# Moving work between VectorE and GpSimd in the opening of a gated attention and feed-forward block, with side operands in PSUM

## What is computed

```python
# step 1: x and the context are quantised to 0..255, then multiplied
q = clip(round(v / s + z), 0, 255);  fake_quant(v) = (q - z) * s
x = x + tanh(g_xattn) * (fake_quant(layernorm(x)) @ fake_quant(ctx))      # ctx: 2 x 1024 x 1024
# step 2: feed-forward with quantised activations and weights
g = max(|a|) / (448 * 6)
A = blockwise fp8 of (a / g), blocks of 16; the last 128 columns twice: value, and what rounding left
W = blockwise int4 of the weights: s = max|w| / 7 per block of 16, round(clip(w / s)) * s
h = silu(A @ Wg.T * g) * (A @ Wu.T * g)                                   # 2752 columns
y = quantised(h) @ Wd.T * g_h
x = x + tanh(g_ffn) * y
```

## Time and profile before

| | us |
|---|---|
| median of 3 runs (892.26 to 893.98) | 892.41 |
| the profiled execution | 893.12 |
| its span, first to last instruction | 891.3 |
| PE busy | 744.3 (84%) |
| DVE busy | 639.3 (72%) |
| POOL busy | 306.9 (34%) |
| ACT busy | 293.8 (33%) |

### The profile page before, as it was taken

How to read it: one execution, slowest core, us unless ns; L and a number is a source line. 1 busy time by engine, 2 the same in 40 slices (tenths; PEclk the granted TensorE clock), 3 DMA queues, 4 the chain that set the end, 5 groups by cost and what they waited for, 6 DMA issues and landing times.

```text
span 891.3 us, 10314 instructions
## 1 busy us (share of the span) xinstructions
PE 744.3 (84%) x3479; PEld 337.1 (38%) x3483; DVE 639.3 (72%) x993; ACT 293.8 (33%) x351; POOL 306.9 (34%) x175
## 2 busy tenths in 40 slices
PE   1697004198589999999999999999699899999998
PEld 0243002044234444444444444444234344444443
DVE  6989999998546575757566675643489999989810
ACT  5753543333214242435252433420122221121100
POOL 2331416525326484757475766640000000000000
PEclk9899557599799999999999999999999999999999
DMA  8630556343478879888987979770524557654420
GB/s 321 224 116 1 116 214 136 67 100 71 105 179 167 192 171 194 172 210 194 203 176 188 217 168 232 169 158 24 197 36 119 129 152 175 141 141 127 112 58 24
DMA packets 228612, 131.37 MB, mean 147 GB/s; under 512 B 201568, under 2 KB 212832, under 8 KB 227552
## 3 DMA queue, kind: packets, MB, share of 16 engines
q1 hardware_dynamic: 228576, 130.92, 60.2%
HBM read 61.88 MB, written 19.66 MB: 91 GB/s over the span
## 4 chain that ended last, share of the span: by engine, by line
PE 68%; DVE 20%; DMA 3%; SPq 2%; issue 2%; ACT 2%; POOL 2%; DVEq 0%; ACTq 0%
PE acc L1096 43%; PE acc L1148 23%; DVE big L1477 1%; DVE bst L1192 1%; SPq L422 1%; DVE h_in L1293 1%; DVE big L1487 1%; DMA mid<-wbuf 1%; DVE big L1479 1%; DVE big L1486 1%; PE acc L1051 1%; DVE w_max L1269 1%; DVE big L1488 1%; POOL big L667 1%; DVE big L1225 1%
## 5 line engine op out<-in xcount | busy, mean ns | idle before, releaser
L1096 PE MATMUL acc<-mid 128*128 128x512 f16 (+1 forms) x2112 | 455.4, 379 | 69.9 <-DMA mid<-big 63.1
L1096 PEld LDWEIGHTS acc<-mid 128*128 128x128 f16 x2112 | 208.8, 99 | 316.2 <-issue 51.2
L1148 PE MATMUL acc<-big,mid 128*128 128x512 f16 x1056 | 232.1, 383 | 9.7 <-DMA mid<-wbuf 8.5
L1148 PEld LDWEIGHTS acc<-big,mid 128*128 128x128 f16 x1056 | 103.7, 99 | 137.5 <-issue 9.1
L706 POOL TENSOR_TENSOR h_in<-wbuf,h_in 128x1024 f16<-128x1024 f32 (+1 forms) x56 | 114.5, 2044 | 107.4 <-ACT h_in L954 107.3
L656 POOL TENSOR_TENSOR wbuf<-wbuf,w_inv 128x1024 f32<-128x1024 f32 (+1 forms) x67 | 129.4, 1939 | 51.6 <-DVE w_inv L1275 51.6
L1506 DVE SCALAR_TENSOR_TENSOR h_out<-acc,gs,silu 128x256 f32<-128x256 f32 (+1 forms) x88 | 41.8, 475 | 124.6 <-ACT silu L881 101.1
L1269 DVE TENSOR_REDUCE tb<-wbuf 128x64 f32<-128x1024 f32 (+1 forms) x60 | 70.3, 1172 | 44.3 <-DMA wbuf<-in_L_ffn_w_gate_dram 28.7
L781 ACT ACTIVATE wbuf<-wbuf 128x1024 f32<-128x1024 f32 (+1 forms) x67 | 68.0, 1016 | 97.8 <-POOL wbuf L656 97.1
L954 ACT ACTIVATE h_in<-wbuf 128x1024 f16<-128x1024 f32 (+1 forms) x56 | 57.0, 1019 | 114.8 <-DVE wbuf L1281 114.8
L1281 DVE SCALAR_TENSOR_TENSOR wbuf<-wbuf,tb 128x1024 f32<-128x1024 f32 (+1 forms) x60 | 69.8, 1166 | 0.2
(11 more groups left out here) (155 smaller groups left out, 525.8 us busy)
## 6 DMA issues: line engine op xcount, KB each, us to landing
h_in<-h_d SPq DMA_DIRECT2D x8, 1376.0 KB, 7.0
wbuf<-in_L_ffn_w_gate_dram SPq DMA_DIRECT2D x21, 512.0 KB, 4.3
wbuf<-in_L_ffn_w_up_dram SPq DMA_DIRECT2D x21, 512.0 KB, 4.3
h_d<-h_out SPq DMA_DIRECT2D x80, 128.0 KB, 3.4
big<-in_ctx_dram SPq DMA_DIRECT2D x16, 512.0 KB, 5.1
wbuf<-in_L_ffn_w_down_dram SPq DMA_DIRECT2D x16, 512.0 KB, 4.4
big<-in_x_dram SPq DMA_DIRECT2D x8, 512.0 KB, 5.8
x_d<-big SPq DMA_DIRECT2D x8, 512.0 KB, 4.1
```

Source lines behind the costliest of these rows:

```text
L1096: last = pe.matmul(acc[m % 4][:, 0:cols], left[:, k, s * P:(s + 1) * P], ring[:, slot, right, k, 0:cols], start=(k == 0 and left is a_hi a ...
L1148: last = pe.matmul(acc[2 * i + hf][:], amT[:, i, k // DH, left, k % DH, :], right[:, k, hf * MW:(hf + 1) * MW], start=(k == 0 and left == ...
```

## The change

Outside the tail's small changes, only the opening is rewritten:

- `clip_ctx` leaves VectorE; GpSimd clips and shifts all 16 context tiles (`clip_shift_ctx`).
- `back_open` of the 11 opening pieces leaves VectorE. ScalarE subtracts the rounding constant (`whole_w`, a new pass), GpSimd multiplies the block scale (`back_open`, a new pass).
- The last multiplication of `end_a` leaves VectorE for GpSimd (`scale_a`).
- `mga`, `a_coef`, `mgo_a` and `omx` of the activations, and the maximum of `front`, lie in PSUM banks (`tb`). A bank holds 512 columns, so `start_a`, `floor_a` and `end_a` work in halves. `a_coef` holds four tiles at a time.
- The P pieces get a place of their own, `p_ring`, in the first three tiles of x; these must have been stored before (`X1_FIRST`, `x1_gone`). Pieces 7 to 10 are then transposed without waiting for P7.
- `nat_a` has four slots, and high and low halves of an activation tile go in one transpose.
- The opening's tiles come as P0, P1, U0, U1, P2, P3, U2, U3 and so on.
- All five lists are in another order: SP issues context and x in turn, then weight pieces 0 to 3 among the context loads; VectorE runs `front_open(0)` to `front_open(10)` before the first pair of tiles is finished.
- VectorE reads one flag early and the other only in the tail.

```diff
-OPENING = (("P", 0), ("P", 1), ("P", 2), ("P", 3), ("U", 0), ("U", 1), ("U", 2), ("U", 3),
-           ("P", 4), ("P", 5), ("U", 4), ("U", 5), ("P", 6), ("P", 7), ("U", 6), ("U", 7))
+OPENING = tuple((kind, t) for q in range(NT // 2) for kind in "PU" for t in (2 * q, 2 * q + 1))
+X1_FIRST = 3
...
+        p_ring = big[:, 0:KT * 2 * PW].bitcast(F16).rearrange("p (v k n) -> p v k n", v=2, k=KT)
+        a_coef = tb[2][:, 0:NT // 2 * NBA].rearrange("p (t b) -> p t b", t=NT // 2)
+        mgo_a = tb[3][:, 4 * NBA:4 * NBA + 2 * SELECT].rearrange("p (s n) -> p s n", s=2)
+        omx_a = tb[3][:, NBA:NBA + 6 * SELECT // BLK].rearrange("p (i n) -> p i n", i=3)
...
+            def load_piece(n):
+                if n >= 4:
+                    sp.wait_ge(nat_lo, n - 3)
...
-                for v, a in enumerate((a_hi, a_lo)):
-                    sp.dma_start_transpose(a[:, :, t * P:(t + 1) * P], nat_a[:, t % 2, v, :]).then_inc(a_across[t % 2], 16)
+                sp.dma_start_transpose(a_both[:, :, t * P:(t + 1) * P], nat_a[:, t % 4, :, :].rearrange("p v h -> p (v h)"))\
+                    .then_inc(a_across[t % 4], 16)
...
+            def clip_shift_ctx(c):
+                w = ctx_buf[c % CTX_BUFS]
+                pool.wait_ge(ctx_affine, c + 1)
+                pool.tensor_scalar(w, w, 255.0, MAGIC, ALU.min, ALU.add).then_inc(ctx_round, 1)
+                pool.wait_ge(ctx_round, c + 1)
+                pool.tensor_scalar(ctxq[:, c, :], w, nmrz[:, 1:2], 1.0, ALU.add, ALU.mult).then_inc(ctx_quant, 1)
...
+            def back_open(n):
+                b = buf(n)
+                pool.wait_ge(w_whole, n + 1)
+                w = blocks(wbuf[:, b, :])
+                pool.tensor_tensor(w, w, spread(w_max[:, b, :]), ALU.mult).then_inc(w_back, 1)
+            def scale_a(t):
+                pool.wait_ge(a_whole, t + 1)
+                v = blocks(xn_all[:, t, :])
+                pool.tensor_tensor(v, v, spread(a_scale[:, t, :]), ALU.mult).then_inc(a_scaled, 1)
...
+            def whole_w(n):
+                b = buf(n)
+                act.wait_ge(w_rounded, n + 1)
+                act.activation(wbuf[:, b, :], wbuf[:, b, :], ACT.Copy, bias=-MAGIC).then_inc(w_whole, 1)
...
+            def start_a(t):
+                dve.wait_ge(ro_ready, t + 1)
+                for hf in range(2):
+                    v, nb = xn_all[:, t, hf * MW:(hf + 1) * MW], MW // BLK
+                    last = dve.scalar_tensor_tensor(out=blocks(v), in0=spread(a_coef[:, t % 4, hf * nb:(hf + 1) * nb]),
+                                                    scalar=gs[:, 6:7], in1=blocks(v), op0=ALU.min, op1=ALU.mult)
+                step(last)
...
+                for hf in range(2):
+                    v = xn_all[:, t, hf * MW:(hf + 1) * MW]
+                    dve.tensor_scalar(tb[hf][:].bitcast(I32), v.bitcast(I32), 0x7F800000, 0x00400000, ALU.bitwise_and, ALU.bitwise_or)\
+                        .then_inc(a_magic, 1)
+            def end_a(t):
+                for op1 in (ALU.add, ALU.subtract):
+                    for hf in range(2):
+                        v = xn_all[:, t, hf * MW:(hf + 1) * MW]
+                        if op1 is ALU.add:
+                            dve.wait_ge(a_floor, 2 * t + (hf + 1))
+                        last = dve.scalar_tensor_tensor(out=v, in0=tb[hf][:], scalar=MAGIC_FLOOR, in1=v, op0=ALU.add, op1=op1)
+                    if op1 is ALU.add:
+                        step(last)
+                last.then_inc(a_whole, 1)
```

More of the change, by code:

```diff
@@ L685, in _ @@
+            back_open(7)
+            lo_open(6)
+            scale(9, 2)
+            back_open(8)
+            scale_a(0)
+            lo_open(7)
+            back_open(9)
+            scale_a(1)
+            lo_open(8)
+            scale(10, 3)
+            lo_open(9)
+            lo_a(0)
+            scale_a(2)
+            scale(11, 0)
+            lo_a(1)
+            back_open(10)
+            scale_a(3)
+            lo_open(10)
             lo_a(2)
+            scale_a(4)
             lo_a(3)
-            lo_open(5)
@@ L894, in _ @@
+            hi_open(6)
+            keep_outliers(1)
+            keep_outliers(2)
+            keep_outliers(3)
+            round_w(8, 1)
+            floor_a(0)
+            hi_open(7)
+            whole_w(8)
+            round_w(9, 2)
+            whole_w(9)
+            hi_open(8)
             floor_a(1)
-            for t in range(4, NT):
-                base(t)
+            hi_open(9)
+            floor_a(2)
+            round_w(10, 3)
             hi_a(0)
+            keep_outliers(4)
@@ new lines, in _ @@
+            dve.tensor_reduce(gmx[:, 0:1], gpart[:, 0:2], AX_X, ALU.max).then_inc(part_max, 1)
+            front_open(8)
+            dve.wait_ge(xn_ordered, 1)
+            with dve.If(in_moved > 0):
+                link = q_link(0)
+                for t in range(NT):
+                    last = dve.tensor_reduce(bmx[:, t, :], blocks(xn_all[:, t, :]), AX_X, ALU.max, apply_absolute_value=True)
+                link(last)
+                a_coef_unbound(slice(0, 4), link)
+                dve.sem_clear(q_step)
```

868 lines of the change are left out of this document (457 added, 411 removed).

## The result

The changed kernel takes **882.71 us** (median of 4 runs, 881.51 to 884.12) against 893.1 us (892.26 to 893.98) of the kernel before on the same chip: a ratio of 0.9884, 95% interval 0.9864 to 0.9905, or 10.4 us less. Forecast were 24.4 us less, 868.0. The sign is right and the time lies in the range, but more than half of the expected gain is missing.

A forecast was written before the change was run, and what follows sets the result against it. The opening's chain DVE, ACT, POOL, SP, PE delays a PE-bound loop. First fold at 151.6, PE at 159.7, loop start at 237.8 instead of 262.8 (-25.0), tail +0.6: -24.4, so 868.0 us; range 848 to 884.

The forecast's parts named there:

- POOL gets 16 clips at about 1.12 (as the shift): Opening, GpSimd: each of the 16 context clips was priced like the shift pass, about 1.12 us.
- The cover that I named: Opening: context done near 58 us stays hidden, as the first weight scale waits for VectorE's front 0 near 78.
- the slower one: Rival, opening: VectorE's small instructions queue behind GpSimd in full, 53 us instead of 10.5, giving 911 us; chance 0.05.
- 16 clips x 0.722 = -11.6: VectorE's list before the first fold: 16 clips gone, making the fold 11.6 us earlier.
- +10.5: VectorE before the first fold: small instructions blocked behind GpSimd add 10.5 us, bounds -3.5 and +45.
- Late weights: VectorE before the first fold: fronts 6 to 10 wait for weight pieces, +4 us, bounds 0 and 10.
- The halves: VectorE's activation passes split in two: start_a costs 2.5 us instead of 1.93, end_a 2.6 instead of 2.5.
- The opening's tiles: PE's 16 opening tiles: 74.6 us without waits, plus 1.5 for tile 1 and 2 for small mismatches.
- Small instructions that hardly wait: Rival, opening: VectorE's small instructions hardly wait and weights are on time, terms -3.5 and 0, giving 850 us; chance 0.20.
- The march: Opening's pairs: VectorE and PE each take 18.2 us per pair; rival: it breaks, 3.5 us more each, 878.5; chance 0.17.
- PSUM does not free VectorE: Rival, opening: VectorE passes with PSUM operands still cost 2.3 to 2.95 us, giving 901 us; chance 0.03.
- PE starting after 185: Sign against the forecast: PE's first opening tile, expected near 160 us, begins after 185.

The follow-up runs named there:

- e2: The changed kernel with GpSimd's clip pass multiplying by 1.0 instead of taking the minimum, so the upper clip is left out; 860.37 us.
- e1: The changed kernel with the 16 context clips back on VectorE and GpSimd only shifting; 860.76 us.
- e10: e2 with context and x loads ahead of the weights and the fourth normalisation's intermediate in PSUM; upper clip left out; 851.85 us.
- e8: e1 with context and x loads ahead of weight pieces and the fourth normalisation's small intermediate in PSUM; 854.23 us.
- e5: e1 with the back passes of the eleven weight pieces on VectorE again, whole_w and back_open gone; 875.46 us.
- e4: The changed kernel with the exponent operand of start_a and end_a in SBUF again, still in halves; 899.41 us.

## Why the prediction was wrong, step by step

**The step that failed** is "POOL gets 16 clips at about 1.12 (as the shift)" and what followed from it, "the context takes 16 x 2.25 = 36 us [...] to about 58: hidden". The pass takes 3.73 us, 16 x 2.6 = 42 us more, and the context is done at 91.2. The cover that I named was front 0 "near 78", 20 us wide; 91.2 is beyond it. Front 0 moved to 95.08, 17 us late, and the first fold ended at 172.1 instead of 151.6. I had taken one row for another because shape and name of the instruction agree, while one of its two operations does not; no row of the trace before had POOL take a minimum, so the term needed a bound from above, and I gave it none. No rival had it either: the slower one put the loss into small instructions.

The cover was mistaken too, and not only too short. On VectorE's list front 0 stands right behind the second `col_lo`, which needs the column sums up to the last context tile. It waited 5.58 us for them and ran at 93.64, and front 0 followed at 95.08. So a late context moves front 0 itself. A list with front 0 ahead of that `col_lo` was not run.

**With that price granted**, the rest of the sum stands against e2, 860.4 measured for 868.0 forecast, 7.6 us too high:
- First fold: 151.6 forecast, 148.13 + 0.42 = 148.6 in e2, though not for the reasons given. "16 clips x 0.722 = -11.6" was an illusion: e1, which keeps them on VectorE, has its fold at 149.0. That VectorE's list got shorter by them bought next to nothing, since it waited for arrivals instead (5.0 us for x in e2 against 0.8 in e1) and its passes met a busier POOL; where the context came early (e10 against e8) it bought 0.7 us at the start of the loop. On the other side, "+10.5" for small instructions was too much. In the changed kernel the first normalisation met no blocking at all, the longest of the second and third were 0.89 and 0.90 us, of the fourth 1.33, 1.78 and 2.05; with one of 0.54 and one of 0.87 these seven stand some 7 us above their free length of 0.17, where before four stood 5.0 above it: 0.90, 1.78 and 2.10, and a second 0.90 in the second normalisation, at 39.20, which those rows leave out. So the term was nearer to +2 than to +10.5. Late weights cost 2.8 us of the 4. The start was right: +6 forecast, and the instruction that stood at 14.49 stands at 20.76.
- From fold to PE: 8.05 forecast, 180.04 - 172.11 = 7.93 in the changed kernel.
- The halves: `start_a` 2.5 forecast, 1.40 + 1.29 = 2.7; `end_a` 2.6 forecast, 2.55. Both whatever POOL did.
- The opening's tiles: 74.6 + 1.5 + 2 forecast, 75.3 measured in the changed kernel. 384 columns take (226.72 - 218.92) / 48 = 0.1625 us, as worked out by width. The two allowances for tile 1 and for mismatches were not needed.
- Back passes: -4.0 in the ledger for the three before the old first fold; e5 gives 14.7 us for all eleven.
- Loop and tail: 374.8 and +0.6 forecast; the loop took 373.1, as no fall of the clock stands at its start. The tail took 0.3 more than before in the changed kernel and 0.9 less in e2, so no run shows what the flag load does there.

**The rivals.** Small instructions that hardly wait were near the truth as a term (+2), but the weights were late by 2.8 us, and e2's 860.4 lies between this rival's 850 and the forecast. The march did not break (0.48 us of waiting in all pairs). Small instructions queued far less than in full. That PSUM does not free VectorE is refuted by e4. For the exponent cut I had 1.2 us a tile and the trace has 2 x 0.69 = 1.38. The rule quoted against the change, that an fp32 pass loses its doubled rate with PSUM (the Trainium skill, "VectorE: DVE Perf Modes", Why PSUM operands drop a tier), had given an estimate of 1.3, nearer than mine; the trace agrees with it, since the same half takes 0.42 us from SBUF to SBUF.

**What I had said would prove it wrong**: PE starting after 185, a wait of over 5 us within a pair, a loop not 374.8 long. Only the last came true, by 1.7 us to the kernel's good, and that was the clock at the loop's start. PE's start, which I wanted "near 160", came at 180.04: past the sign for right, short of the sign for wrong, so 185 was too loose to catch the failing step. POOL busy from 78 to 160 was seen in the main, 66.3 of 82 us with 14.5 of waits for DVE's fronts, and from 10 on as well, 78.4 of the 81.2 us to the end of the context. Small instructions of over 1 us were seen in the fourth normalisation alone.

## What to carry to other kernels

Before work goes to another engine, look for a row of *that engine* doing *that operation*; shape and instruction name are not enough, and where there is no row the term gets a bound from above, and the cover beneath it is tested against that bound. Moving work off a busy engine pays only if that engine is not waiting for arrivals in the same stretch: here 16 clips were worth 0.4 us, or 0.7 before the loop with the context early, and 11 later passes 15 us. When several edits come as one, undo them one at a time: one part was worth -22 us and two others +17 and (with the first undone) +15, and the sum showed only 10.
